# Norm of the four-layer graph network: constant factors prepared once, the first turned block cut in two, and one product moved behind the last sums

## The reference

```python
for i in range(N_LAYERS):                      # 4 layers
    agg = segment_sum(h[src], dst)             # sum over the edges
    z = agg + h
    z = relu(z @ W1[i] + b1[i]) @ W2[i] + b2[i]
    mean = mean(z, axis=0); var = var(z, axis=0)        # per feature, over all nodes
    z = (z - mean) * rsqrt(var + BN_EPS) * gamma[i] + beta[i]
    h = relu(z)
```

## Time and profile before

| | |
|---|---|
| time, median of 3 | 1241.56 us (1241.06 to 1241.62) |
| profiled execution | 1241.05 us, span of its instructions 1239.4 us |
| TensorE busy | 1130.0 us, 91% of the span, 6308 products |
| VectorE busy | 684.7 us, 55% |
| ScalarE busy | 452.7 us, 37% |
| GpSimd busy | 11.9 us, 1% |
| granted TensorE clock, mean | 0.975 of full speed |
| chain that ended last | TensorE 80%, VectorE 11%, ScalarE 3% |

### The profile page before, as it was taken

How to read it: one execution, slowest core, us unless ns; L and a number is a source line. 1 busy time by engine, 2 the same in 40 slices (tenths; PEclk the granted TensorE clock), 3 DMA queues, 4 the chain that set the end, 5 groups by cost and what they waited for, 6 DMA issues and landing times.

```text
span 1239.4 us, 19336 instructions
## 1 busy us (share of the span) xinstructions
PE 1130.0 (91%) x6308; PEld 659.1 (53%) x6308; DVE 684.7 (55%) x2174; ACT 452.7 (37%) x1334; POOL 11.9 (1%) x37
## 2 busy tenths in 40 slices
PE   1677899999998999999899899898699999999997
PEld 1556667665464564644545445444555456554644
DVE  8999999996553225545346255255645324632311
ACT  1557988896573112211311301311522123820100
POOL 1000000000000000000000000000100000000000
PEclk9999899999999999999899899899799999999999
DMA  3100000001001013524133133299922213510001
GB/s 67 30 2 1 2 2 10 2 2 41 11 4 27 17 27 69 108 58 92 31 68 74 32 86 78 58 201 201 246 63 72 90 48 81 133 42 25 11 26 30
DMA packets 208306, 70.33 MB, mean 57 GB/s; under 512 B 180999, under 2 KB 207306, under 8 KB 208203
## 3 DMA queue, kind: packets, MB, share of 16 engines
q1 hardware_dynamic: 119995, 41.90, 15.0%
q10 hardware_dynamic: 87840, 25.80, 9.6%
q0 software_dynamic: 368, 1.34, 0.4%
HBM read 20.71 MB, written 28.26 MB: 40 GB/s over the span
## 4 chain that ended last, share of the span: by engine, by line
PE 80%; DVE 11%; ACT 3%; issue 2%; DMA 2%; DVEq 0%; SPq 0%; ACTq 0%; POOL 0%; POOLq 0%
PE PS L1180 51%; PE PS L889 8%; DVE HPb L753 4%; PE PS L2502 4%; PE PS L1501 2%; PE PS L878 2%; PE PS L854 2%; PE PS L1979 2%; PE PS L1973 2%; DVE HPb L704 2%; DMA deg_d<-ADJ 1%; PE PS L2009 1%; PE PS L1225 1%; DMA HPb<-s_d 1%; DVE ADJ L718 1%
## 5 line engine op out<-in xcount | busy, mean ns | idle before, releaser
L1180 PE MATMUL PS<-ADJ,HPb 125*128 125x500 bf16 (+2 forms) x2350 | 471.6, 355 | 4.5 <-DVE HPb L1367 2.7
L1180 PEld LDWEIGHTS PS<-ADJ,HPb 125*128 125x128 f16 x2350 | 228.6, 98 | 241.7 <-issue 35.8
L925 ACT CAST ADJ<-PS 126x72 f32 (+7 forms) x784 | 193.5, 316 | 51.8 <-PE PS L889 18.4
L1180 PE MATMUL PS<-ADJ,Zf 125*128 125x500 bf16 (+2 forms) x1050 | 202.1, 352 | 0.0
L889 PE MATMUL PS<-HPb 128*128 128x150 bf16 (+3 forms) x784 | 194.0, 351 | 2.6 <-ACT ADJ L925 1.9
L1180 PEld LDWEIGHTS PS<-ADJ,Zf 125*128 125x128 f16 x1050 | 102.4, 97 | 93.8 <-issue 1.3
L753 DVE TENSOR_SCALAR HPb<-XRf,Zf 128x176 bf16<-128x176 f16 (+2 forms) x588 | 135.1, 289 | 1.3 <-PE PS L889 0.4
L878 PEld LDWEIGHTS PS<-HPb 128*128 128x128 bf16 x642 | 87.2, 142 | 61.1 <-issue 34.2
L1774 DVE CUSTOM_DVE_ANT_0 HPb<-ADJ,HPb 125x625 bf16<-125x625 bf16 x125 | 101.2, 810 | 3.7
L878 PE MATMUL PS<-HPb 128*128 128x25 bf16 x642 | 91.1, 215 | 12.8 <-DVE HPb L753 12.0
L1873 DVE TENSOR_SCALAR Zf<-PS,B_L 128x500 f32<-128x500 f32 (+2 forms) x28 | 19.1, 682 | 141.5 <-PE PS L1979 141.5
(11 more groups left out here) (331 smaller groups left out, 1035.5 us busy)
## 6 DMA issues: line engine op xcount, KB each, us to landing
adj_d<-ADJ ACTq DMA_DIRECT2D x25, 700.0 KB
HPb<-y_d SPq DMA_DIRECT2D x19, 187.5 KB, 2.6
HPb<-di_d SPq DMA_DIRECT2D x10, 250.0 KB, 3.4
adj_d<-ADJ ACTq DMA_DIRECT2D x25, 81.2 KB
ADJ<-in_x SPq DMA_DIRECT2D x1, 1562.5 KB
q_d<-HPb SPq DMA_DIRECT2D x25, 62.5 KB
HPb<-di_d SPq DMA_DIRECT2D x5, 305.2 KB
HPb<-s_d ACTq DMA_DIRECT2D x5, 250.0 KB, 3.9
```

The source lines that it names most:

```text
L925: e.copy(to, WPS[group % BANKS][0:PD, t0 * RESTS[q]:t1 * RESTS[q]] .rearrange("p (t d) -> p t d", t=t1 - t0)).then_inc(s_mv, 1)
L1180: mm = e.matmul(accs[q], H[0:PN, t, q, 0:P], cols, start=(t == 0 and (two or q == 0)), stop=(t == NT - 1 and (two or q == 1)), skip_group_ ...
```

## The change

Three edits, all in the four-layer network.

1. **Factors known beforehand.** gamma and beta, each multiplied with the factor 1/CF of the layer (RS; 1.0 for the last layer), and gamma negated are computed once for all four layers, ahead of the layers. At a boundary BNA and the negated factor BNT then come from the reciprocal in two instructions with no wait between them, and BNB = mean * BNT + beta in one more. The copy of CF goes ahead of the wait for the square root.
2. **First block in two.** BLOCKS is (2 tiles), (3 tiles), and four blocks of 5; NBL = 6 is their number. It holds for the boundaries between layers; the last layer keeps its five blocks. Semaphore values are counted accordingly.
3. **Output product behind the last sums.** `outputs(5)`, in each layer, no longer stands ahead of source tile 11 of chunk 6's sums, but behind the last of them, ahead of `hidden(6)`.

```diff
@@ set-up
+    BLOCKS = [(0, 2), (2, BT - 2)] + [(b * BT, BT) for b in range(1, NB)]
+    NBL = len(BLOCKS)
@@ VectorE, ahead of the layers
+                line(e.memset(RS[:, LAYERS - 1:LAYERS], 1.0))
+                line.sync()
+                for to, q in ((GAMMA, Q_GA), (BETA, Q_BE)):
+                    line(e.tensor_tensor(to, B_L2[:, q, :], RS[:, 0:LAYERS], ALU.mult))
+                line.sync()
+                line(e.tensor_scalar(GAMMA_NEG, GAMMA, -1.0, None, ALU.mult))
                 line.sync()
@@ layer2, VectorE
                     e.sem_inc(s_bn["var"], 1)
+                    if not last:
+                        line(e.tensor_copy(CF, SDV[:, l:l + 1]))
                     e.wait_ge(s_bn["sd"], l + 1)
                     line(e.reciprocal(BNR, BNS))
                     line.sync()
-                    line(e.tensor_tensor(BNA[:, 0:1], BNR, bias2(Q_GA, l), ALU.mult))
-                    line.sync()
-                    line(e.tensor_tensor(BNT, BNM[:, 0:1], BNA[:, 0:1], ALU.mult))
-                    line.sync()
-                    line(e.tensor_tensor(BNB[:, 0:1], bias2(Q_BE, l), BNT, ALU.subtract))
-                    line.sync()
-                    if not last:
-                        up = RS[:, bass.ds(l, 1)]
-                        line(e.tensor_tensor(BNA[:, 0:1], BNA[:, 0:1], up, ALU.mult))
-                        line(e.tensor_tensor(BNB[:, 0:1], BNB[:, 0:1], up, ALU.mult))
-                        line(e.tensor_copy(CF, SDV[:, bass.ds(l, 1)]))
-                        line.sync()
+                    line(e.tensor_tensor(BNA[:, 0:1], BNR, GAMMA[:, l:l + 1], ALU.mult))
+                    line(e.tensor_tensor(BNT, BNR, GAMMA_NEG[:, l:l + 1], ALU.mult))
+                    line.sync()
+                    line(e.scalar_tensor_tensor(out=BNB[:, 0:1], in0=BNM[:, 0:1], scalar=BNT, in1=BETA[:, l:l + 1],
+                                                op0=ALU.mult, op1=ALU.add))
+                    line.sync()
                     e.sem_inc(s_bn["ab"], 1)
...
@@ layer2, ScalarE
                     def relu(b):
-                        zb = Zf[:, b * BT * PN:(b + 1) * BT * PN]
+                        j, n = blocks_of(l)[b]
+                        zb = Zf[:, j * PN:(j + n) * PN]
@@ next_span
+                starts = {j: b for b, (j, n) in enumerate(BLOCKS)}
                 def before(t):
-                    if t % BT == 0:
-                        if t // BT + 1 < NB:
-                            turn_block(l, t // BT + 1)
-                        done(E2["hp"], l * NB + t // BT + 1)
+                    if t in starts:
+                        if starts[t] + 1 < NBL:
+                            turn_block(l, starts[t] + 1)
+                        done(E2["hp"], l * NBL + starts[t] + 1)
@@ rest_of_layer
-                        if t == 11:
+                        if t == 11 and c < NC - 1:
                             outputs(c - 1)
...
                     sum_span(l, c, before)
+                outputs(NC - 2)
                 hidden(NC - 1)
                 outputs(NC - 1)
```

More of the change, by code:

```diff
@@ L1082, in degree_rows @@
                 e.wait_ge(s_dout, 118)
-                e.wait_ge(s_bn["tr"], LAYERS * NB)
+                e.wait_ge(s_bn["tr"], (LAYERS - 1) * NBL + NB)
                 for c in range(NC - 1):
@@ L1126, in block @@
             def block(b):
-                t = slice(b * BT, (b + 1) * BT) if isinstance(b, int) else bass.ds(b * BT, BT)
+                t = slice(BLOCKS[b][0], sum(BLOCKS[b]))
                 return Zn[0:PN, t, :], HP[0:PN, t, 0, 0:P], HP[0:PN, t, 1, 0:P]
@@ L1740, in layers @@
                 rows_out(s1_d, DEG)
+            GAMMA, GAMMA_NEG, BETA = (NBI[:, k * LAYERS:(k + 1) * LAYERS] for k in range(3))
             def bias2(q, l):
@@ L1860, in close_row_sums, with blocks_of @@
                 e.sem_inc(s_dout, 1)
+            def blocks_of(l):
+                return BLOCKS if l < LAYERS - 1 else [(b * BT, BT) for b in range(NB)]
             def layer2(l, last):
@@ L1867, in layer2 @@
                     else:
-                        done(E2["hp"], l * NB)
+                        done(E2["hp"], l * NBL)
                     settle()
@@ L1902, in layer2 @@
                     else:
-                        for b in range(NB):
-                            low_part("L2", b, l * NB + b + 1, turned_block(b))
+                        for b in range(NBL):
+                            low_part("L2", b, l * NBL + b + 1, turned_block(b))
                 if act:
@@ L1923, in relu @@
                     def relu(b):
-                        zb = Zf[:, b * BT * PN:(b + 1) * BT * PN]
+                        j, n = blocks_of(l)[b]
+                        zb = Zf[:, j * PN:(j + n) * PN]
                         e.activation(zb, zb, ACT.Relu, bias=BNB[:, 0:1], scale=BNA[:, 0:1]).then_inc(s_bn["rel"], 1)
                     relu(0)
-                    for b in range(NB):
-                        if b + 1 < NB:
+                    for b in range(len(blocks_of(l))):
+                        if b + 1 < len(blocks_of(l)):
                             relu(b + 1)
                         if not last:
-                            e.wait_ge(s_bn["tr"], l * NB + b + 1)
+                            e.wait_ge(s_bn["tr"], l * NBL + b + 1)
                             high_part("L2", b, turned_block(b))
@@ L2002, in turn_block @@
             def turn_block(l, b, ring=RB):
-                e.wait_ge(s_bn["rel"], l * NB + b + 1)
+                e.wait_ge(s_bn["rel"], l * NBL + b + 1)
                 if b >= len(ring):
-                    done(E2["hp"], l * NB + b + 1 - len(ring))
-                for m in range(BT):
-                    c = (b * BT + m) * PN
+                    done(E2["hp"], l * NBL + b + 1 - len(ring))
+                j, n = blocks_of(l)[b]
+                for m in range(n):
+                    c = (j + m) * PN
                     mm = e.transpose(ring[b % len(ring)][0:PN, m * P:(m + 1) * P], Zf[:, c:c + PN], IDF[:, :])
@@ L2073, in third_high @@
                     third_root(0)
-                    e.wait_ge(s_bn["tr"], (LAYERS - 1) * NB + 2)
+                    e.wait_ge(s_bn["tr"], (LAYERS - 1) * NBL + 2)
                 e.wait_ge(s_rs3, b + 1)
@@ L2100, in layers @@
             if general and pe:
-                done(E2["hp"], LAYERS * NB)
+                done(E2["hp"], (LAYERS - 1) * NBL + NB)
                 with e.Fori(0, NT * NT) as m:
```

4 lines of the change are left out of this document (2 added, 2 removed).

## The result

The changed kernel takes 1239.66 us (median of 22 runs, 1237.89 to 1244.8) where the kernel before takes 1242.68 us (22 runs, 1239.57 to 1247.05). The ratio is 0.9974 with a 95% interval of 0.9964 to 0.9984: 3.2 us faster, 2.0 to 4.5 with the interval. The forecast was 5.0 us less than the 1241.56 us that three runs had shown; in these 22 the kernel before stands 1.1 us higher. A second set of runs gave 0.9968 (0.9950 to 0.9985). The first three runs stood within 0.6 us of each other, and the 22 do not: single runs differ by several us, so in what follows the parts of the program are compared by their own length in the profiles, and whole times only by their ratio.

What follows compares the result with a forecast made beforehand. TensorE's waits in the data-forced chain at layer ends were taken as the bound; 2.0 + 1.55 + 1.8 = 5.4 us, less 0.4 for the clock, took 1241.05 to 1236.05, forecast as 1236.5 us for the median, range 1233.5 to 1239.3.

Steps and rivals of the forecast that it cites:

- Step A: End of each layer's sums: with chunk 5's output product moved behind them, `hidden(6)` starts 0.5 us earlier, four times, 2.0 us.
- Step B: Reciprocal to relu at layer ends: precomputed factors save 0.47 us three times and 0.14 us in the last layer, 1.55 us.
- Step C: Relu to first sum at three boundaries: the split shortens 4.04 to 2.37 us, net 0.61 us each, 1.8 us.
- The clock: From first transpose to clock rise at three boundaries: rise mostly follows the work, so only 0.4 us is taken off.
- Rival (1): Layer ends: the clock's rise stays in place, or the output product's gain is lost; 3.0 us gained, about 1238.5 us; chance 0.18.
- Rival (2): Pauses before the boundary transposes: the clock no longer falls, 5 us more gained, 1231 us; chance 0.08.
- Rival (3): Boundary transposes: thinner work makes the clock rise later, costing 7.2 us, 1243.7 us; chance 0.04.
- Rival (4): Layer ends: factors and split shorten links hidden by something else; gain under 2.5 us, 1240 us; chance 0.08.

Runs made afterwards that it cites:

- The hold: Changed kernel with SyncE's last two transposing DMAs held until GpSimd's six degree rows have landed: 1236.05 us, ratio 0.9948 to the kernel before.

## Why the prediction was wrong

The direction was right, and so were the waits at the layer end and what shortened them. The size was not: 5.0 us forecast, 3.2 us measured, and 1239.66 us lies just above the range's 1239.3. Three things make up the 3.2 us between the forecast 1236.5 and 1239.66. The kernel before stands at 1242.68 us instead of 1241.56, 1.1 us that the change has nothing to do with; with the ratio 0.9974 on 1241.56 the time would have been 1238.3. The stage gained 4.3 us instead of 5.0. And behind the last layer part of that was given back, 1.1 us by the ratio (1.3 by the medians), 2.5 in four profiles.

**Step A**, the output product, was right: 0.50 us measured in each layer, 0.5 forecast. The margins named for it held: `keep` cost hundredths and became visible in the chain.

**Step B**, the factors: 0.39 us instead of 0.47, since the last step takes 0.23 and not 0.16 us. I had priced a scalar_tensor_tensor by the rows of two-operand instructions. Over the layers that is 1.2 us instead of 1.55.

**Step C**, the split: relu to first sum was met (2.37 us). The cost of the moved transposes was met too (1.07 us, 1.06 forecast). The slope of 0.82 ns per column that it used for the relu comes from none of its rows, which give 0.6; the measured 0.60 us for 250 columns bears it out.

**The clock.** A, B and C as measured make 2.0 + 1.2 + 1.8 = 5.0 us, and the stage shrank by 4.3 us; the clock took 0.7, where I had taken off 0.4. I had read the 4.8, 4.8 and 5.4 us from first transpose to rise as a rise that follows the work. The changed kernel has 3.4 to 6.2 us in its first profile and 4.1 to 6.5 in two more, so it does not follow closely.

**The failed step** is the overlap behind the last layer: "SyncE's two transposing DMAs are issued as chunk 6's sums end at 861.52 us and fill 36 us, and they also start 0.64 us earlier." From it the sum let the whole gain of the stage through to the end and put the loss there at nothing. The trigger did move along with everything else, 6.2 us ahead of the first transposes in both kernels, but the degree rows that GpSimd issues in the middle of these DMAs took 14.5 us instead of 11.3 to reach VectorE, and TensorE came to wait 2.14 us for the first product that needs them. In the earlier trace rows the two DMAs stand as one bar of 36 us, and I did not ask who else needed the DMA engines under it, though the chain before already ran through a DMA of 8.4 us there. The hold shows it: without these DMAs in flight the wait is gone and the stretch is 4.1 to 4.3 us shorter. Their length is not what counts: with the pauses filled they took 36.3 us, about as before, and the wait was the longest, 3.50 us. Why the rows land later in the changed kernel, although everything in the tail starts in the same relation, is open; in the profiles it goes with the split. The program could also be less exposed: VectorE waits for all six rows ahead of the first multiplication, which reads only the first. That one landed 7.9 us after its issue, more than 2 us before the sums were done. No run tried a wait for it alone.

**Rivals.** Rival (1) had the right size (3.0 us) by luck: A came whole, the clock took 0.7 us where a rise in place would have taken 2.4, and the rest went where no rival looked. Rival (2), the clock no longer falling, did not happen in the changed kernel, though in one of the three pauses of each of its profiles it fell only when the transposes had begun. Its price was about right: 3 x 1.7 = 5 us estimated, 6.1 measured with the pauses filled. Rival (3) did not happen: 6.8 us is the longest slow stretch from a first transpose to the rise in any profile. Its evidence was also weaker than it looked: the unbroken transposes behind the last layer, with which the clock stayed down before, are followed by a rise at 866.2 us in the changed kernel. (Its threshold, 5.0 / 3 x 2, is 3.3 us and not 3.4.) Rival (4) did not happen: B and C came nearly whole.

## What to carry to other kernels

Follow a gain past the place where it arises, to the next point where engines meet a DMA: ask which transfers are in flight there, who shares the DMA engines with them, and which of them is needed first. Long transfers that are needed late can be held until short ones that are needed at once have landed, but look at what they meet then. And where TensorE's clock falls in a wait that the data force, filling the wait can be worth more than shortening it: three times 14 idle products took 6.1 us off the stage, the three edits 4.3.

## What was not expected of the hardware

The same two transposing DMAs took 36.2 to 40.4 us of SyncE's queue when issued at the end of the last layer, and 28.2 to 34.1 us when issued behind the degree rows. The row loads among them landed in a median of 8.0 us in the kernel before and 10.6 in the changed one, and in 4.8 with the two DMAs held. The granted clock fell between 1.4 and 4.1 us after the last product of a layer, in the same code (nine layer ends in three profiles), and once it had fallen it rose 3.4 to 6.5 us after the first transpose: the same kernel's layers took 88.13, 86.13 and 87.41 us, and with the clock kept up 85.62, 84.98 and 84.99. Whole times of one kernel spread over 7 us in 22 runs, where the first three agreed to 0.6.
